# Two normalized convolutions: another lead, statistics exchanged through memory, and the 5x5 code entered later

## The reference, cut to what matters

```python
def _gn(v, G=16, eps=1e-05):             # normalized over 2 channels x H x W
    g = v.reshape(B_, G, C_ // G, H_, W_)
    m = jnp.mean(g, axis=(2, 3, 4), keepdims=True)
    s = jnp.var(g, axis=(2, 3, 4), keepdims=True)
    return ((g - m) / jnp.sqrt(s + eps)).reshape(v.shape)

x = x + conv3x3(_gn(x), weight * mask(weight, threshold))     # x: (16, 32, 128, 128) float32
x = x + conv5x5(_gn(x), kernel) + bias
```

## Time and profile before

| | |
|---|---|
| median of 3 runs | 880.9 us (880.46 to 882.7) |
| the profiled execution | 882.4 us, of which the span is 880.6 us |
| granted TensorE clock, mean over the span | 0.964 |
| busy, share of the span | PE 90%, PEld 80%, DVE 77%, ACT 37%, POOL 36% |
| matmuls | 52300 |
| DMA | 150.52 MB, mean 171 GB/s |

### The profile page before, as it was taken

How to read it: one execution, slowest core, us unless ns; L and a number is a source line. 1 busy time by engine, 2 the same in 40 slices (tenths; PEclk the granted TensorE clock), 3 DMA queues, 4 the chain that set the end, 5 groups by cost and what they waited for, 6 DMA issues and landing times.

```text
span 880.6 us, 108990 instructions
## 1 busy us (share of the span) xinstructions
PE 789.2 (90%) x52300; PEld 705.5 (80%) x52300; DVE 679.1 (77%) x989; ACT 326.0 (37%) x417; POOL 317.3 (36%) x154
## 2 busy tenths in 40 slices
PE   1673579999999999999999999999999999998884
PEld 1552368888989889899888888988989889987773
DVE  5576378979898989989897989898998878664210
ACT  0122024344344444344434434444434443433331
POOL 1020004444433333334434444333334444443332
PEclk9887789999999999999999999999999999999998
DMA  8954965969787787868696868878795556454222
GB/s 178 211 120 116 221 153 135 234 144 225 172 215 201 198 207 188 218 168 223 151 236 144 221 178 206 211 196 208 182 220 157 158 147 160 107 136 114 66 56 56
DMA packets 83843, 150.52 MB, mean 171 GB/s; under 512 B 20960, under 2 KB 28384, under 8 KB 79712
## 3 DMA queue, kind: packets, MB, share of 16 engines
q1 hardware_dynamic: 79200, 145.92, 67.7%
q10 hardware_dynamic: 4608, 4.23, 1.9%
HBM read 75.60 MB, written 33.59 MB: 124 GB/s over the span
## 4 chain that ended last, share of the span: by engine, by line
PE 77%; DVE 10%; issue 4%; SPq 3%; DMA 2%; ACTq 1%; ACT 1%; DVEq 1%; POOL 0%; POOLq 0%
PE psum L711 76%; DVE x L572 3%; SPq L225 2%; DMA x_bands<-x_dram 2%; DVE bn_in L498 1%; DVE x_bands L557 1%; ACTq L398 1%; DVE bn_out L600 1%; DVE mid L592 1%; DVEq L595 1%; DVE mid_bands L557 1%; SPq L220 0%; DVE product L530 0%; POOL mid L322 0%; DVE deviation L534 0%
## 5 line engine op out<-in xcount | busy, mean ns | idle before, releaser
L322 POOL TENSOR_TENSOR mid<-mid,conv_out 128x512 f32<-128x512 f32 x128 | 308.0, 2437 | 502.4 <-ACT conv_out L355 489.1
L711 PE MATMUL psum<-x_hi,s 32*32 32x512 f16 x25600 | 378.0, 382 | 21.4 <-issue 9.7
L711 PEld LDWEIGHTS psum<-x_hi,s 32*32 32x32 f16 x25600 | 343.0, 88 | 47.3 <-issue 16.6
L711 PE MATMUL psum<-x,s 32*32 32x512 f16 x13824 | 228.9, 391 | 28.0 <-DVEq L595 14.7
L711 PEld LDWEIGHTS psum<-x,s 32*32 32x32 f16 x13824 | 176.4, 88 | 78.9 <-issue 49.2
L711 PE MATMUL psum<-x_lo,s_hi 32*32 32x512 f16 x12800 | 186.1, 376 | 3.5 <-issue 3.3
L711 PEld LDWEIGHTS psum<-x_lo,s_hi 32*32 32x32 f16 x12800 | 175.8, 88 | 8.4 <-issue 4.6
L580 DVE TENSOR_TENSOR x_lo<-mid_bands,x_hi 128x2560 f16<-128x2560 f32 x32 | 102.3, 3197 | 59.4 <-PE psum L711 59.0
L572 DVE TENSOR_TENSOR x<-x_bands,x 128x2304 f16<-128x2304 f32 x32 | 100.6, 3144 | 35.2 <-PE psum L711 35.2
L355 ACT ACTIVATE conv_out<-psum,bias,unscale 128x512 f32<-128x512 f32 x128 | 94.4, 769 | 60.1 <-PE psum L711 60.0
L364 ACT ACTIVATE s<-s_lo 128x800 f16<-128x800 f16 x32 | 27.9, 871 | 179.3 <-PE psum L711 179.3
(11 more groups left out here) (74 smaller groups left out, 175.1 us busy)
## 6 DMA issues: line engine op xcount, KB each, us to landing
x_own<-x_dram SPq DMA_DIRECT2D x128, 256.0 KB
mid_bands<-mid SPq DMA_DIRECT2D x512, 64.0 KB
out_dram<-mid SPq DMA_DIRECT2D x128, 256.0 KB
x_bands<-x_dram SPq DMA_DIRECT2D x96, 288.0 KB, 6.1
x_bands<-x_dram SPq DMA_DIRECT2D x32, 272.0 KB, 7.4
mid_bands<-mid SPq DMA_DIRECT2D x224, 32.0 KB
every_mv<-mv_scratch ACTq DMA_DIRECT2D x16, 256.0 KB
w<-L_conv_kernel_dram SPq DMA_DIRECT2D x4, 100.0 KB, 18.6
```

The lines of the kernel that those rows point to most:

```text
L322: nc.gpsimd.tensor_tensor(m, m, conv_out[:, b, :], ALU.add).then_inc(out_added, 1)
L711: ins = nc.tensor.matmul(psum[quad(j), bank + i, :].rearrange("p (a w) -> p a w", a=A), w[quad(i), at, :], src[quad(i), A * j + dy:A * (j ...
```

## The change

It has five parts.

1. Only the statistics of image 0 still go through PE. Those of x of image 1, of mid of image 0 and of x of image 2 are exchanges 1, 2 and 3 through memory. The sums over partitions for the weights, formerly matmuls with a matrix of ones, are a multiplication, a 32x32 transpose and a reduction on DVE. The bound of the 5x5 weights is taken before the first take_conv3.
2. normalize moves from DVE to ACT, as an Identity activation with scale and bias; DVE makes the bias (gshift) and still clears the padding rows. Only the first half is normalized by DVE.
3. SP moves the edge pieces of an image before the 16 pieces of its second half (move_edges takes a source and a target), and loads bands 5 before it waits for the first mid.
4. On DVE the order in a step is now the same in odd and even steps, without the normalizing.
5. PE: the lead's code is also used by step 3 up to its first 3x3 products; then comes a lead_first5, and the loop's code is entered at inner5. keep_warm is called with 18, and with 9 twice a step, in place of 11 and 6.

```diff
-            def move_edges(n):
+            def move_edges(n, source, to):
+                sp.wait_ge(mid_made, PIECES * (2 * n + source + 1))
...
             load_bands(4)
+            load_bands(5)
             move_mid(0)
             load_own(2)
+            move_edges(0, 1, 0)
             move_mid(1)
-            move_edges(0)
-            load_bands(5)
+            load_own(3)
+            move_edges(0, 0, 1)
             load_bands(6)
-            load_own(3)
+            load_bands(7)
             move_mid(2)
-            load_bands(7)
...
                 if has3(s):
+                    if s % 2:
+                        move_edges(s // 2, 1, 0)
+                        move_edges(s // 2, 0, 1)
                     move_mid(s)
-                    if s % 2:
-                        move_edges(s // 2)
...
+            def normalize(which, h):                       # on ACT
+                act.wait_ge(landed[h % slots], 16 * each * (h // slots + 1))
+                act.wait_ge(scale_ready, ROOTS.index((("x", "mid")[which], h // 2)) + 1)
+                nc.scalar.activation(v, v, ACT.Identity, bias=gshift[:, at], scale=gscale[:, at]).then_inc(made, 1)
...
             take_root(("x", 0))
             high3(0)
-            for s in range(STEPS + 1):
+            for s in range(LAG):
+                act.wait_ge(c3_early, 3 * s + 1)
+                weights3(s3_lo, 0, 1)
+                act.wait_ge(c3_inner, 3 * s + 1)
+                weights3(s3_lo, 1, 1)
+                if s == 0:
+                    spread_stats(X1_EXCHANGE)
+                if s == 1:
+                    take_root(("x", 1))
+                if s == 2:
+                    spread_stats(MID0_EXCHANGE)
+                act.wait_ge(c3_whole, 2 * s + 1)
+                weights3(s3_hi, 0, 2)
+                weights3(s3_hi, 1, 2)
+                if s == 0:
+                    normalize(0, 1)
+                    gather_stats(X1_EXCHANGE)
+                if s == 1:
+                    normalize(0, 2)
+                if s == 2:
+                    gather_stats(MID0_EXCHANGE)
+                    normalize(0, 3)
+                high3(s + 1)
+                if s == 2:
+                    take_root(("mid", 0))
+                    normalize(1, 0)
+                    high5(0)
+            for s in range(LAG, STEPS + 1):
...
+                if s == LAG:
+                    spread_stats(X2_EXCHANGE)
+                    gather_stats(X2_EXCHANGE)
+                elif has3(s + 1):
+                    normalize(0, s + 1)
...
                 if has3(s + 1):
                     high3(s + 1)
+                if has5(s + 1):
+                    normalize(1, s + 1 - LAG)
...
             low3(0)                                        # on DVE
-            normalize3(1)
-            mean_of(("x", 1))
-            take_conv3(0)
-            variance_of(("x", 1))
-            scale_of(("x", 1))
-            stats_out(0)
             dve.wait_ge(w_loaded, 16 * 2 * Q)
             largest(w5, 1)
+            power_of_two(1)
+            nc.vector.memset(carrier[:, 0:1], 0.0).then_inc(w5_bounded, 1)
+            clear_pad(0, 1)
+            take_conv3(0)
+            dve.wait_ge(mix_loaded, 16)
+            dve.wait_ge(mv_in, 16 * X1_EXCHANGE)
+            group_stats(("x", 1))
+            scale_of(("x", 1))
+            stats_out(0, range(0, 2))
             low3(1)
...
             low3(2)
-            normalize3(3)
-            variance_of(("mid", 0))
+            clear_pad(0, 3)
+            stats_in(4, range(BANKS))
+            dve.wait_ge(mv_in, 16 * MID0_EXCHANGE)
+            group_stats(("mid", 0))
             scale_of(("mid", 0))
-            normalize5(0)
             take_conv3(2)
...
             with nc.body("lead_low", valid_engines=only):
-                pe.br_eq(step, 0, on_true="lead_low0", on_false="lead_low12")
+                pe.br_eq(step, LAG, on_true="lead_first5", on_false="lead_gap")
+            with nc.body("lead_gap", valid_engines=only):
+                keep_warm(9)
+                pe.br("lead_inner3")
...
+                keep_warm(9)
+                pe.br("lead_first3")
+            with nc.body("lead_first5", valid_engines=only):
+                first5()
+                pe.br("hot")
+            nc.switch_bb("hot")
             pe.addr_align(256, offset=0, max_nops=0)
-            pe.br("first3")
+            pe.br("inner5")
             with nc.body("first3", valid_engines=only):
                 hint = pe.mark_branch_hint_location()
```

More of the change, by code:

```diff
@@ L628, in _ @@
             stats_in(3, range(BANKS))
[L629 removed]
+            aggregate("x", 1, mv_ready)
             low3(0)
[L632 to L637 removed]
             dve.wait_ge(w_loaded, 16 * 2 * Q)
             largest(w5, 1)
+            power_of_two(1)
[7 more added lines that the diff above has]
+            stats_out(0, range(0, 2))
             low3(1)
[L641 to L643 removed]
+            stats_out(0, range(2, BANKS))
+            clear_pad(0, 2)
             take_conv3(1)
             stats_out(1)
[L646 to L647 removed]
+            aggregate("mid", 0, mv_ready)
             low3(2)
[L649 to L650 removed]
+            clear_pad(0, 3)
+            stats_in(4, range(BANKS))
+            dve.wait_ge(mv_in, 16 * MID0_EXCHANGE)
+            group_stats(("mid", 0))
             scale_of(("mid", 0))
[L652 removed]
             take_conv3(2)
[L654 to L655 removed]
+            clear_pad(1, 0)
             stats_in(5, range(BANKS))
             aggregate("x", 2, mv_ready)
[L658 to L660 removed]
+            low3(LAG)
+            low5(0)
+            stats_out(2)
+            dve.wait_ge(mv_in, 16 * X2_EXCHANGE)
+            group_stats(("x", 2))
+            scale_of(("x", 2))
+            take_conv3(LAG)
+            clear_pad(0, LAG + 1)
+            stats_in(6, range(BANKS))
+            stats_out(LAG)
+            clear_pad(1, 1)
+            stats_in(7, range(BANKS))
+            aggregate("mid", LAG // 2)
+            aggregate("x", (LAG + 3) // 2, mv_ready)
+            stats_in(8, range(BANKS))
+            for s in range(LAG + 1, STEPS):
                 gathered = exchanged(s - 1)
@@ L666, in _ @@
                     low3(s)
-                if s == LAG:
-                    dve.wait_ge(mv_in, 16)
-                    group_stats(("x", 2))
-                    scale_of(("x", 2))
                 if has3(s + 1):
-                    normalize3(s + 1)
-                if has5(s + 1) and s % 2:
-                    normalize5(s + 1 - LAG)
-                if s == LAG:
-                    stats_in(6, range(BANKS))
-                if gathered and s > LAG:
+                    clear_pad(0, s + 1)
+                if gathered:
                     dve.wait_ge(mv_in, 16 * exchange_number(s - 1))
@@ L682, in _ @@
                     take_conv3(s)
-                if has5(s + 1) and not s % 2:
-                    normalize5(s + 1 - LAG)
                 if has3(s):
                     stats_out(s)
-                if s == LAG:
-                    stats_in(7, range(BANKS))
+                if has5(s + 1):
+                    clear_pad(1, s + 1 - LAG)
                 if exchanged(s):
@@ L701, in _ @@
         def _(pe):
-            def over_partitions(bank, src):
-                nc.tensor.matmul(psum[:, bank, 0:1], ones[:, :], src, start=True, stop=True).then_inc(w_summed, 1)
             def tap(w, at, src, t, k, bank, start=False):
@@ L816, in _ @@
             pe.reg_mov(visit5, 0)
+            pe.wait_ge(ones_set, 1)
+            pe.wait_ge(mix_loaded, 16)
+            mix_mean(("x", 0))
+            mix_variance(("x", 0))
+            keep_warm(18)
+            pe.wait_ge(w3b_go, 1)
             pe.br("lead_first3")
```

158 lines of the change are left out of this document (59 added, 99 removed).

## The result

| | before | changed |
|---|---|---|
| median | 880.68 us (878.21 to 882.7, 4 runs) | 904.92 us (904.3 to 911.1, 4 runs) |
| ratio | | 1.0292 (95%: 1.024 to 1.0344) |
| the profiled span | 880.6 us | 902.8 us |

What follows compares the result with a forecast made beforehand. PE was taken as the bound in steps 4 to 31. Span 880.6 - 2.2 (lead) - 4.2 (normalizing on ACT) + 16 (jump past the hint) = 890.2 us, median 890.5; own range 883 to 899, with first rival 872 to 899.

Steps and rivals of the forecast that it cites:

- The jump past the hint: Step 3 enters low_image without the hint; PE fetches a ninth block, pushing out the first, once around: 16 us lost.
- 14.7, and 1.7 more: Refetch round behind step 3: 14.7 us of block stalls, plus 1.7 us for the slower clock.
- After a stall of 4.4 us the clock was 0.60 for the next 4 us ... 1.7 more: Clock term of the refetch round: 128 matmuls in 3.52 us instead of 1.8, so 1.7 us more.
- The three rivals that made it cheap: Ninth block harmless, 874.5 us (0.22); only block 1 refetched, 882 us (0.12); first fetches meet a light queue, 880 us (0.08).
- The lead: Everything before step 4: step 4 was to start 2.2 us earlier, from 13 us earlier to 7 us later.
- low3 of step 1 starts as late as before: Exchange of x of image 1: slow gather wait of 11.7 us assumed, so low3 of step 1 gains nothing.
- 8, 7, 7 and 4.5 us and 1.5 us for the rest: Step 3's entry at inner5: prices for fetching blocks 2 to 5 in turn, first inner5 ending at 112 us.
- The rest of step 3 goes as before: Step 3 behind its first inner5: the two stalls of 1.7 and 1.6 us stay.
- Normalizing on ACT: Steps 4 to 31: with 63 passes fewer DVE is never late for low3, 4.2 us gained; the passes fit on ACT.
- a lead that gets full queues on top of a full refetch: Case left out of the 872 to 899 us range, together with a light queue without refetch, some 15%.

Runs made afterwards that it cites:

- run 1: Changed kernel with the branch hint moved from first3 to last5, so step 3 executes it too: 886.33 us, ratio 1.0027 to the kernel before.
- run 4: The kernel before with its marker and branch hint removed, nothing else: 1420.35 us, one run.
- run 10: Run 7's code once more (entry at first3, load_bands(5) later), on one chip with 8 and 9: 869.46 us, ratio 0.9883 to the kernel before.
- run 2: Changed kernel with step 3 entering the loop at first3, over the hint, rest of the new lead kept: 876.77 us, ratio 0.9932 to the kernel before.
- run 5: Run 2 with normalizing put back on DVE from step 4 on: 879.7 us, ratio 0.9986 to the kernel before.
- 8: Run 2's code once more, on one chip with 9 and run 10: 874.96 us, ratio 0.9938 to the kernel before.
- 9: Run 5's code once more (normalizing on DVE from step 4 on), on one chip with 8 and run 10: 878.24 us, ratio 0.9972 to the kernel before.
- run 3: Run 1 with load_bands(4) issued behind move_mid(0) and load_bands(5) behind move_edges(0, 1, 0): 882.09 us, ratio 1.0 to the kernel before.
- run 7: Run 2 with only load_bands(5) issued later, behind load_own(3): 873.37 us, median of four, ratio 0.9887 to the kernel before.

## Why the prediction came out as it did

*The jump past the hint: right mechanism, too small.* Of "14.7, and 1.7 more" for the clock, the stalls were near in their sum, 4.24 + 1.49 + 4.12 + 2.67 + 1.74 + 1.61 = 15.9 us, but partly by luck. Blocks 1 and 2 were to cost 5.9 and 1.9 us and cost 4.24 and nothing visible; blocks 3, 4 and 5 were to cost 0, 1.8 and 1.8 and cost 1.49, 4.12 and 2.67. The 1.8 was a price for light queues, and from 153 to 159 us, where block 4 was waited for, the DMA engines' share was 1.04. The clock was wrong in size. The granted clock fell to half, the 1.2 GHz level, twice, each time while PE stood still, once in the 4.24 us stall and once in the 4.12 us one, and stayed there for the matmuls behind:

```profile
141.00:148.00 7.00, 4.12 (x160) 2.88 (x170) 1.62 (x1) 0.98 (x2) 3.34 (x2) 0.51 0.33 78
158.20:168.40 10.20, 6.46 (x239) 4.35 (x247) 0.00 (x0) 0.86 (x2) 0.00 (x0) 0.50 0.70 172
```

The 288 matmuls took 6.36 us instead of 4.57, 127 took 3.64 instead of 2.04, the 55 behind them 1.90 instead of 1.06, and the 144 then 2.94 instead of 2.25: 4.9 us in place of 1.7. Some 1.2 us of the step's 22.0 are left, which are not placed. The failed step is "After a stall of 4.4 us the clock was 0.60 for the next 4 us ... 1.7 more": the price of one drop was charged once for the whole round, whose list had one stall of over 4 us (block 1). The round had two, since block 4 was priced as with light queues, and the clock stayed low over more matmuls than the 128 of that row. The three rivals that made it cheap fell: the ninth block does harm (run 1 against the changed kernel), more than block 1 is fetched (eight packets), and the queue was not light. The one rule of the Trainium skill that the prediction leaned on ("Runtime: NRT & Kernel Launch", the section on instruction fetch: a first-in-first-out store of eight blocks) is borne out in its size by run 4, where nine packets a step follow from nine blocks in a store of eight. The order is not told by it: a store that pushes out the block used longest ago would give nine packets too. The section's other sentence, on branches outside two blocks, is not borne out: the changed kernel ran 639 us of an eight-block loop without a fetch.

*The lead: -2.2 forecast, +6.3 measured.* Three steps of it failed, and one sum was wrong. First, "low3 of step 1 starts as late as before": it started at 56.86 instead of 52.34. The row of DVE's wait in the changed kernel is

```profile
52.67 0.38 DVE L588 SCALAR_TENSOR_TENSOR product<-every_mv,mix 128x128 f32<-128x128 f32 x1 [9.24 <-DMA every_mv<-mv_scratch]
```

and in run 10, with the loads of bands 5 moved behind the exchange,

```profile
46.36 0.49 DVE L588 SCALAR_TENSOR_TENSOR product<-every_mv,mix 128x128 f32<-128x128 f32 x1 [3.78 <-DMA every_mv<-mv_scratch]
```

I had taken the slow value for the gather alone, 11.7 us, but an exchange is two transfers in a row. ACT issues the gather only when the spread has landed:

```profile
30.83 0.35 ACTq L387 DMA_DIRECT2D mv_scratch<-mv  x1
39.88 0.33 ACTq L392 DMA_DIRECT2D every_mv<-mv_scratch  x1
```

The numbers came at 52.6, 12.7 us after the gather's issue. In run 10 the gather was issued at 39.86 and the numbers came at 46.3, 6.5 us later, so it is the second transfer that bands 5 held up. Step 3 thus started at 82.66 instead of my 78, and its first 3x3 products were done at 88.6 instead of 85, though step 0 had ended 2.7 us earlier than before (40.8 against 43.5), which the forecast did not have. PE had keep_warm matmuls to do ahead of the first code stall, and its issue wait was 3.0 us where 5.1 had been. Second, "8, 7, 7 and 4.5 us and 1.5 us for the rest", taken as 27 us from there to the end of the first inner5 (85 to 112): it took 117.9 - 88.6 = 29.3. These terms add up to 28 and not 27, so 1 us of this miss is a slip in the sum: the forecast should have read -1.2 us for the lead and 891.5 for the median. From one block's arrival to the next it took 5.9, 8.4, 5.0 and 8.5 us. Third, "The rest of step 3 goes as before": step 3's last two stalls were 4.16 + 0.85 us, not the 1.7 + 1.6 of before, with the clock at 0.58 between them. So 3.6 + 2.3 + 2.6 = 8.5 us, which is the miss. Run 2 shows how to see the same sum from the other side: the new lead without the entry at inner5 is 1.5 us shorter than the old, and the entry alone costs 7.8. I had charged the entry, but not that step 3 would reach its last blocks with the queues still full: around the stall of 4.16 us the DMA engines' share was 0.96 (127 to 131 us), and around that of 1.7 us before it was 0.22 (124 to 128 us). This third part is not the entry's, since run 2 has a stall of 4.11 us at the same place.

*Normalizing on ACT: right in kind, and in size as far as the runs tell.* Steps 5 to 31 are 3.2 us shorter, with no wait for low3 any more. Putting the passes back on DVE gives 1.2 us of this back in the profiles of 2 and 5, 2.0 us in those of 8 and 9, and 3.3 us in the medians of 8 and 9; whether the rest comes from the other order of DVE's work or from the edge pieces is not shown. The passes took 2.3 and 2.5 us where 2.12 and 2.4 were taken:

```profile
L352 ACT ACTIVATE mid_bands<-mid_bands,gshift,gscale 128x2560 f32<-128x2560 f32 x32 | 80.6, 2518 | 2.5 <-DVE gshift L609 2.5
...
L352 ACT ACTIVATE x_bands<-x_bands,gshift,gscale 128x2304 f32<-128x2304 f32 x31 | 71.6, 2311 | 2.8 <-DVE gshift L609 2.1
```

*Not in the sum at all:* the tail's clock, -2.9 us by chance. Without it the miss would have been 3 us larger. The span was forecast at 890.2 us; 8.5 for the lead, 6.0 for step 4 and 1.0 for the smaller gain on ACT, less 2.9, make the 902.8 measured.

*The range.* Its upper end took in 7 us for a bad lead on top of the forecast, and left out "a lead that gets full queues on top of a full refetch". That is what happened. I take the two as not independent, since both are code blocks that are fetched beside the same loads; no run separates them.

## What to carry to other kernels

A loop that fills an engine's instruction store exactly stands or falls with what is fetched after its last block. If a hint on the closing branch is what protects it, as here, every way into the loop must execute the hint before the last block is entered; a shortcut past it cost a whole round (22 us here), and a missing hint one round per turn (1420 us instead of 881). Enter such a loop at its first block, and look for the code queue's packets in the first turn and behind it.

A tiny exchange through memory is two transfers in a row, and each can be held up by large loads. For x of image 1 the second took 12.7 us, and 6.5 with the loads of bands 5 behind it (run 10). For mid of image 0 the first took 2.6 us in the changed kernel, and 7.9 in run 3, where bands 4 and 5 ran beside it. Place the large loads behind the exchange that is waited for, and then look which later exchange they meet instead: of two placements that both cured the first wait, one put 8 us of wait on the next exchange and the other none.

## What the runs showed of the hardware

- Rounds of stalls cost twice: in step 4 the granted clock fell to half in two stalls of a little over 4 us and was still at half for 4 us of matmuls behind the first and for 9 us, with another stall among them, behind the second, so that 15.9 us of stalls made a step 22 us longer.
- The same 2.9 us gap dropped the clock in some executions and not in others (400 matmuls in 5.7, 7.4 or, in run 7, 8.65 us). The three such stretches of the tail took 17.2 us in run 5 and 24.2 in run 7.
- A hint placed in last5, near the loop's end, protected the loop as well as one in its first block, but let a round of nine packets into the tail of one profiled execution of 900 us (run 1); in run 3 it let two packets in.
- A PE loop of eight code blocks ran without a fetch from 186 to 825 us when the hint on its closing branch was executed in every turn, and with nine packets and 43.2 us a turn without the hint (run 4).
- A scaled and shifted ACT pass over 128x2304 in float32 took 2.31 us where the copy to float16 of the same width takes 2.13.
